# GATv2 and mixture-of-experts layer on one core: the norm's subtraction of one dropped, seven of the late message products moved from VectorE to GpSimd

## The chip, the cores and the metric

One core of one Trainium2 chip runs the whole kernel in one launch. The time is the device time of that core in microseconds (us). Times of separate runs are given as a median with the lowest and the highest run; one further execution was taken with the profiler, and all rows below are from that one.

## What is computed

The input is x of 1250 nodes by 256 features, and 40000 edges sorted by destination. Two residual steps follow each other; the change lies in the first, the graph step:

```python
def _gatv2_block(x, edge_index, W_l, W_r, att, bias, gamma, beta):   # x is already layer-normed
    xl = (x @ W_l).reshape(N, 4, 64);  xr = (x @ W_r).reshape(N, 4, 64)
    e = xl[src] + xr[dst];  e = where(e >= 0, e, 0.2 * e)
    score = einsum('ehd,hd->eh', e, att)
    ex = exp(score - segment_max(score, dst)[dst])
    alpha = ex / (segment_sum(ex, dst)[dst] + 1e-16)
    agg = segment_sum(alpha[:, :, None] * xl[src], dst)
    out = agg.reshape(N, 256) + bias
    h = elu(out) + x
    return (h - mean(h)) * rsqrt(var(h) + 1e-5) * gamma + beta
x = x + _gatv2_block(layernorm(x), ...)
x = x + top2_of_64_experts(layernorm(x))
```

The products alpha * xl[src] are called messages here. elu(out) is max(out, 0) + min(exp(out), 1) - 1.

## The kernel before, in words

The program runs in stages. The node stage norms x and projects it. The graph stage (`graph_phase`) goes over all edges. The route stage (`route_phase`) ends the sum with the bias, forms elu, norms twice, picks experts and scatters the rows to expert slots. The expert stage (`expert_phase`) does the two matrix products of 64 experts and adds up. The graph stage is a block of its own: no engine starts on the route stage before every engine has finished the graph stage.

The edges are cut in tiles of 128, and three tiles make a step: 108 steps (`STEPS`). Nine steps (`GPB`) make a block of the softmax, so there are 12 blocks, numbered 0 to 11. The last block but one is block 10, steps 90 to 98; the last block is steps 99 to 107. Each engine runs a loop over 108 + 20 loop steps (`STEPS + LAG`) with an order written out by hand:

- GpSimd only gathers: three indirect DMAs per step bring the rows xl[src] into the ring `G` of 26 steps (L131). The gathers for the last step are issued about 20 loop steps before the end; from then on GpSimd has nothing in the graph stage.
- TensorE at loop step s forms xl[src] + xr[dst] of step s in PSUM (`expand`, L689 to L696), turns the softmax's rows and columns of the block before (`turn_scores` to `turn_alpha`, L714 to L734), and aggregates step s - 20 (`aggregate`, L707): three matmuls by the one-hot matrix `M`, each of which the trace shows as two records, into `agg`, which fills five banks of PSUM. From loop step 108 there is nothing more to expand.
- ScalarE evacuates PSUM (L783, L784), takes the exponent of the scores (`exps`, L788), copies the weights alpha into `A` (`copy_alpha`, L794), and forms the third of a step's three messages, head by head (`weigh_head`, L805), one loop step ahead of TensorE.
- VectorE builds one-hots (L848), multiplies by att and reduces (L854, L862), runs the softmax of a block in pieces spread over loop steps k = 2 to 7 of the block after (`local_max` L904, L906, L890; `scan_rows` L896, L898; `full_max` L911 to L915; `local_sum` L920, L890, L922; `full_sum` L926 to L938), forms the first two of a step's messages in one 128x512 product (`weight`, L872), two loop steps ahead of TensorE, and scales the sum of the node that two blocks share (`rescale`, L881).

The ring `msg` holds four steps (`RA`), so the messages of step s may be written once step s - 4 is aggregated (semaphore `agged`). The order within one loop step of TensorE is fixed. At loop step 108 + k, k = 1, 2, 3, 5, 6 and 8, a turn for block 11 stands ahead of, or between, the aggregation of step 88 + k, and what stands behind a waiting turn waits too. In particular `turn_alpha` of block 11 stands ahead of the aggregation of step 96. The aggregation of the first step of a block waits for `rescale`.

Two chores were put in the last loop steps: ScalarE subtracts one from `xn`, the normed x, in five instructions of 128x512 (`lower`, L811 to L813, loop steps 109 to 113), and VectorE adds beta to xs in five (`add_beta`, L885). In the route stage `lift` adds min(exp, 1), max(out, 0) and `xn` (L1199 on GpSimd for all but the first of six groups, L1316, L1323), and the norm behind it subtracts the mean (L1301, L1304, L1332).

Of the kernel before, what the change touches and what calls it, by code (L numbers as in the profile page):

```python
# [23 lines left out]
P = 128  # L24
# [9 lines left out]
U = 3  # L34
# [30 lines left out]
LEAD = 2  # L65
CG = 3
# [473 lines left out]
def graph_phase(nc, v):  # L540
# [5 lines left out]
    with ExitStack() as ctx:  # L546
# [35 lines left out]
        consumed, freed = sem("consumed"), sem("freed")  # L582
        att_mul, scored, weighted, shared, agged = sem("att_mul"), sem("scored"), sem("weighted"), sem("shared"), sem("agged")
        dv = sem("dv_graph")
        init, rows_set, marks_out = sem("init"), sem("rows_set"), sem("marks_out")
# [16 lines left out]
        def by_block(row):  # L602

            return row.rearrange("o (b i) -> o b i", i=B)

# [59 lines left out]
        @block.gpsimd  # L665
        def _(g):

            for s in range(AHEAD, STEPS):
                if GS <= s < RG:
                    g.wait_ge(consumed, s - GS + 1)  # L670
                if s == RG - MG:
                    g.wait_ge(marks_out, 16 * 7)
                if s >= RG:
                    g.wait_ge(freed, s - RG + 2)
                gather_group(nc, G, xl_tab, srcI, gathered, s)

        @block.tensor
        def _(pe):
# [20 lines left out]
            def aggregate(s, u, w):  # L699

                if u == 0:
                    pe.wait_ge(weighted, s + 1)
# [34 lines left out]
            for s in range(STEPS + LAG):  # L737
# [3 lines left out]
                for u in range(U):  # L741
# [4 lines left out]
                    if (s, u) == (1, 0):  # L746
                        pe.wait_ge(init, 1)
# [23 lines left out]
        def _(act):  # L771
# [18 lines left out]
            def copy_alpha(b):  # L790
                act.wait_ge(alpha_ps, b + 1)
                if b >= 2:
                    act.wait_ge(weighted, GPB * (b - 1))
# [17 lines left out]
            def lower(i):  # L811

                nc.scalar.activation(xn[:, 2 * i:2 * i + 2, :], xn[:, 2 * i:2 * i + 2, :], ACT.Copy, bias=-1.0).then_inc(folded, 1)  # L813

            for s in range(STEPS + LAG):
                b, k = s // GPB - 1, s % GPB
                if 0 <= s - STEPS - 1 < NW // 2:
                    lower(s - STEPS - 1)
# [11 lines left out]
            act.wait_ge(folded, NW)  # L830

        @block.vector
        def _(dve):
# [31 lines left out]
            def weight(s):  # L865

                b, k, n = s // GPB, s % GPB, U - 1
                if k == 0:
                    dve.wait_ge(alpha_set, b + 1)
                if s >= RA:  # L870
                    dve.wait_ge(agged, s - RA + 1)
                V.tensor_tensor(msg[:, s % RA, 0:n * D].rearrange("p (q d) -> p q d", d=HD),  # L872
                                G[:, s % RG, 0:n * DX].rearrange("p (q f) -> p q f", f=HX)[:, :, 0:HD],
                                A[:, b % 2, k * U:k * U + n, :].rearrange("p u h -> p (u h)").unsqueeze(2)
                                .broadcast_to([P, n * HEADS, HD]), ALU.mult).then_inc(weighted, 1)
# [145 lines left out]
            dve.sem_inc(init, 1)  # L1021
            early = (clear_tables, mask_tables, end_tables, clear_marks, link_marks, row_marks, penalties, constants)

            for s in range(STEPS + LAG):
# [12 lines left out]
                if 0 <= s - LAG + LEAD < STEPS:  # L1037
                    weight(s - LAG + LEAD)
# [16 lines left out]
            dve.wait_ge(folded, NW)  # L1055
# [823 lines left out]
```

## Time and profile before

| | us |
|---|---|
| median of 3 runs | 880.72 |
| lowest and highest run | 874.63, 883.66 |
| the profiled execution, its own time | 872.36 |
| its span (first to last instruction) | 870.6 |
| TensorE busy in the span | 721.0 (83%) |
| VectorE busy | 560.3 (64%) |
| ScalarE busy | 355.9 (41%) |
| GpSimd busy | 411.5 (47%) |

The span starts at 0. PE is TensorE, PEld its weight loads, DVE is VectorE, ACT ScalarE, POOL GpSimd, SP SyncE. L872 is line 872 of the kernel. Busy time is a sum over a whole program with four stages, so it says nothing about one of them; the rows below are cut by time. The graph stage ends at about 622.6 us, and the part of it that the change touches begins at about 588 us.

### The profile page before, as it was taken

To read this page: it belongs to the slowest core of one execution; us is meant where nothing else is said; L and a number is where in the kernel's file an instruction comes from. 1 tells how busy PE (TensorE), PEld (TensorE's weight loads), DVE (VectorE), ACT (ScalarE), POOL (GpSimd) and SP (SyncE) were. 2 spreads that over 40 slices of the span, in tenths; PEclk is the share of its full clock that TensorE was granted. 3 is DMA by queue.
4 is the path that set the end of the run, shared out by engine and by line. 5 is a ranking of instruction groups with operands and counts; after the bars stand their busy time and mean duration, and the time that the engine had idled before them with its cause. 6 is when DMAs were issued, how large, how long until landed. Compare 5 with 4: busy or idle time off the path is not lost. (4 is left out here: it accounts for less than half of the span.)

```text
span 870.6 us, 14203 instructions
## 1 busy us (share of the span) xinstructions
PE 721.0 (83%) x4151; PEld 490.7 (56%) x4153; DVE 560.3 (64%) x1355; ACT 355.9 (41%) x1256; POOL 411.5 (47%) x405
## 2 busy tenths in 40 slices
PE   4844777997999889988988898998855499999995
PEld 2722444665666666666766565776544255555553
DVE  5653657886778777777876687878697333434333
ACT  1411334554455555555554464657632121121220
POOL 0566666366667656666765566710326011212121
PEclk9975798999999999999998899999955699999998
DMA  4545463344354435353534353510299899999995
GB/s 122 98 156 148 111 170 97 113 114 125 94 150 112 135 90 149 100 144 95 156 95 125 97 139 108 133 30 1 93 411 405 249 317 367 367 369 370 368 390 200
DMA packets 66875, 154.81 MB, mean 178 GB/s; under 512 B 17390, under 2 KB 30142, under 8 KB 66769
## 3 DMA queue, kind: packets, MB, share of 16 engines
q1 hardware_dynamic: 45824, 100.40, 34.2%
q0 software_dynamic: 18384, 51.06, 21.5%
q10 hardware_dynamic: 2592, 2.43, 0.9%
q8 instruction: 40, 0.66, 0.3%
q14 instruction: 35, 0.28, 0.1%
HBM read 138.76 MB, written 15.39 MB: 177 GB/s over the span
## 5 line engine op out<-in xcount | busy, mean ns | idle before, releaser
L131 POOL DMA_INDIRECT G<-xl_tab,srcI x324 | 344.6, 1064 | 196.0 <-issue 80.4
L783 ACT ACTIVATE L<-psE 128x264 f32<-128x264 f32 x324 | 126.4, 390 | 277.6 <-PE psE L696 200.0
L696 PE MATMUL psE<-G,ident 128*128 128x264 f32 x648 | 209.2, 406 | 0.0
L707 PE MATMUL agg<-msg,M 128*128 128x256 f32 x648 | 191.2, 395 | 6.4 <-issue 4.8
L693 PE MATMUL psE<-xr,MT 128*128 x972 | 176.9, 292 | 0.0
L854 DVE TENSOR_TENSOR L<-L,attb 128x792 f32<-128x792 f32 x108 | 105.7, 978 | 93.6 <-ACT M L784 46.5
L689 PE MATMUL psE<-identb,MT 128*128 128x128 bf16 x324 | 74.1, 229 | 81.4 <-issue 39.2
L805 ACT ACTIVATE msg<-G,A 128x64 f32<-128x64 f32 x432 | 136.8, 354 | 1.5 <-PE agg L707 1.2
L707 PEld LDWEIGHTS agg<-msg,M 128*128 128x128 f32 x648 | 118.5, 194 | 33.3 <-issue 17.4
L693 PEld LDWEIGHTS psE<-xr,MT 128*128 128x128 bf16 x972 | 88.5, 101 | 41.7 <-issue 6.0
L696 PEld LDWEIGHTS psE<-G,ident 128*128 128x128 f32 x648 | 105.5, 203 | 5.1
L862 DVE TENSOR_REDUCE S<-L 128x12 f32<-128x792 f32 x108 | 105.7, 978 | 3.4
L689 PEld LDWEIGHTS psE<-identb,MT 128*128 128x128 bf16 x324 | 32.7, 101 | 123.1 <-issue 65.3
L1612 POOL DMA_INDIRECT yk_d<-Y,row x33 | 31.7, 960 | 146.1 <-DVE Y L1769 133.7
L784 ACT COPY M<-psE 128x128 f32<-128x128 f32 x324 | 84.9, 262 | 0.0
L872 DVE TENSOR_TENSOR msg<-G,A 128x512 f32<-128x512 f32 x108 | 74.2, 687 | 2.5 <-PE agg L707 2.1
L1769 DVE COPY Y<-psY 128x256 f32<-128x256 f32 x32 | 13.6, 425 | 90.7 <-PE psY L1666 90.7
L1647 PE MATMUL psH<-w,xT 128*64 128x512 f32 x240 | 59.8, 620 | 0.0
L1661 PE MATMUL psY<-w,hid 128*64 128x256 f32 x480 | 57.0, 379 | 0.5 <-DMA w<-in_L_ffn_W 0.4
L1661 PEld LDWEIGHTS psY<-w,hid 128*64 128x64 f32 x480 | 34.3, 137 | 30.2 <-issue 15.4
L1828 ACT COPY hraw<-psH 128x512 f32<-128x512 f32 x33 | 19.3, 585 | 68.5 <-PE psH L1647 68.5
L1821 ACT COPY xT<-psXe 128x256 f32<-128x256 f32 x33 | 12.3, 372 | 70.8 <-PE psXe L1625 70.8
(302 smaller groups left out, 723.1 us busy)
## 6 DMA issues: line engine op xcount, KB each, us to landing
w<-in_L_ffn_W SPq DMA_DIRECT2D x120, 512.0 KB
relb<-rel_d SPq DMA_DIRECT2D x36, 288.0 KB
G<-xl_tab,srcI POOLq DMA_INDIRECT x324
tabs<-tab_d SPq DMA_DIRECT2D x48, 98.2 KB
X<-xs_d SPq DMA_DIRECT2D x58, 64.5 KB
xn<-in_L_ffn_W SPq DMA_DIRECT2D x6, 512.0 KB
h_in<-in_L_ffn_W SPq DMA_DIRECT2D x6, 512.0 KB
xs_d<-zslot SPq DMA_DIRECT2D x8, 322.5 KB
```

What stands on the lines that cost most here:

```text
L131: nc.gpsimd.indirect_dma_start(out=G[:, g % RG, u * DX:(u + 1) * DX], out_offset=None, in_=xl_tab, in_offset=bass.IndirectOffsetOnAxis(ap= ...
L689: turned = nc.tensor.matmul(psE[:, e, DX:DX + P], mt, identb[:, :], start=True, stop=True)
L693: nc.tensor.matmul(psE[:, e, 0:DX], mt, xr3[:, bass.ds(w * (3 * DX) + j * DX, DX)], start=(j == 0), stop=False)
L696: nc.tensor.matmul(psE[:, e, 0:DX], ident[:, :], G[:, s % RG, u * DX:(u + 1) * DX], start=False, stop=True).then_inc(expanded, 1)
L707: last = nc.tensor.matmul(agg[:, bass.ds(w * D, D)], M[:, s % RM, u * P:(u + 1) * P], msg[:, s % RA, u * D:(u + 1) * D], start=False, stop ...
L783: nc.scalar.activation(L[s % RL][:, u * DX:(u + 1) * DX], psE[:, e, 0:DX], ACT.Relu)
L784: nc.scalar.copy(M[:, s % RM, u * P:(u + 1) * P], psE[:, e, DX:DX + P]).then_inc(evacuated, 1)
L805: last = nc.scalar.activation(msg[:, s % RA, u * D + h * HD:u * D + (h + 1) * HD], G[:, s % RG, u * DX + h * HX:u * DX + h * HX + HD], ACT ...
L854: V.tensor_tensor(every, every, attb[:, :].unsqueeze(1).broadcast_to([P, U, DX]), ALU.mult).then_inc(att_mul, 1)
L862: V.tensor_reduce(S[:, b % 2, :, 1 + k * U:1 + (k + 1) * U].rearrange("p h u -> p u h"), L[s % RL][:, :].rearrange("p (u h f) -> p u h f", ...
L872: V.tensor_tensor(msg[:, s % RA, 0:n * D].rearrange("p (q d) -> p q d", d=HD), G[:, s % RG, 0:n * DX].rearrange("p (q f) -> p q f", f=HX)[ ...
L1661: last = nc.tensor.matmul(psY[part(h), b, 0:D], hid[:, b, m * P + h * CAP:m * P + (h + 1) * CAP], w2[2 * r + h][:, m, :], start=(m == 0), ...
```

## The change

Two edits. `lower` goes, and with it ScalarE's wait at its end; VectorE waits at the end of the stage for its own five `add_beta` alone. The route stage's text does not change: what it adds is now larger by one in every element, and the norm that follows subtracts the mean of the row. And for steps 92 to 98 (`BY_POOL`, the last seven of block 10) the 128x512 product of the first two messages is issued by GpSimd, behind its last gather, with a semaphore of its own (`weighted_p`), instead of by VectorE at loop steps 110 to 116. TensorE waits on the one or the other semaphore. ScalarE still forms the third message of every step. The semaphore `init` is replaced by a third count of `marked`. No DMA is added, removed or moved.

```diff
--- before.py
+++ after.py
@@ -63,6 +63,7 @@
 LAG = 20
 RM, RT, RL, RA = LAG + 2, 4, 3, 4
 LEAD = 2
+BY_POOL = range(STEPS - GPB - 7, STEPS - GPB)
 CG = 3
 CHUNKS, RC = STEPS // CG, 2
 assert STEPS % CG == 0 and RG - LAG <= GS and LAG >= 2 * GPB + LEAD
@@ -579,10 +580,10 @@
         colC, colD, colR, alphaT = psS[0:RB, 368:370], psS[0:RB, 370:372], psS[:, 372:372 + HEADS], psS[:, 384:384 + RB]
 
         onehot, expanded, evacuated = sem("onehot"), sem("expanded"), sem("evacuated")
-        consumed, freed = sem("consumed"), sem("freed")
+        consumed, freed, weighted_p = sem("consumed"), sem("freed"), sem("weighted_p")
         att_mul, scored, weighted, shared, agged = sem("att_mul"), sem("scored"), sem("weighted"), sem("shared"), sem("agged")
         dv = sem("dv_graph")
-        init, rows_set, marks_out = sem("init"), sem("rows_set"), sem("marks_out")
+        rows_set, marks_out = sem("rows_set"), sem("marks_out")
         tab_set, tab_out, marked, ends_in = sem("tab_set"), sem("tab_out"), sem("marked"), sem("ends_in")
         tabs_in = [sem(f"tabs_in{b}") for b in range(2)]
         scores_ps, ends_set, rows_ps, carried, cin_ps = map(sem, ("scores_ps", "ends_set", "rows_ps", "carried", "cin_ps"))
@@ -602,6 +603,18 @@
         def by_block(row):
 
             return row.rearrange("o (b i) -> o b i", i=B)
+
+        def pair_of_messages(eng, s):
+
+            b, k, n = s // GPB, s % GPB, U - 1
+            return eng.tensor_tensor(msg[:, s % RA, 0:n * D].rearrange("p (q d) -> p q d", d=HD),
+                                     G[:, s % RG, 0:n * DX].rearrange("p (q f) -> p q f", f=HX)[:, :, 0:HD],
+                                     A[:, b % 2, k * U:k * U + n, :].rearrange("p u h -> p (u h)").unsqueeze(2)
+                                     .broadcast_to([P, n * HEADS, HD]), ALU.mult)
+
+        def vector_messages(s):
+
+            return s + 1 - len([p for p in BY_POOL if p <= s])
 
         def load_tabs(sp, b):
 
@@ -673,6 +686,11 @@
                 if s >= RG:
                     g.wait_ge(freed, s - RG + 2)
                 gather_group(nc, G, xl_tab, srcI, gathered, s)
+            for s in BY_POOL:
+                if s == BY_POOL[0]:
+                    g.wait_ge(alpha_set, s // GPB + 1)
+                g.wait_ge(agged, s - RA + 1)
+                pair_of_messages(nc.gpsimd, s).then_inc(weighted_p, 1)
 
         @block.tensor
         def _(pe):
@@ -699,7 +717,10 @@
             def aggregate(s, u, w):
 
                 if u == 0:
-                    pe.wait_ge(weighted, s + 1)
+                    if s in BY_POOL:
+                        pe.wait_ge(weighted_p, s - BY_POOL[0] + 1)
+                    else:
+                        pe.wait_ge(weighted, vector_messages(s))
                     if s % GPB == 0 and s > 0:
                         pe.wait_ge(rescaled, s // GPB)
                 if u == U - 1:
@@ -744,7 +765,7 @@
                     if u == 0 and s + 1 < STEPS + LAG:
                         nxt = load_windows(pe, windows[(s + 1) % 2], wrow[0:1, s + 1, :])
                     if (s, u) == (1, 0):
-                        pe.wait_ge(init, 1)
+                        pe.wait_ge(marked, 3)
                         for j in range(NW * D // 512):
                             nc.tensor.matmul(agg[:, j * 512:(j + 1) * 512], zero[:, 0:P], zero[:, :], start=True, stop=False,
                                              skip_group_check=True)
@@ -790,7 +811,7 @@
             def copy_alpha(b):
                 act.wait_ge(alpha_ps, b + 1)
                 if b >= 2:
-                    act.wait_ge(weighted, GPB * (b - 1))
+                    act.wait_ge(weighted, vector_messages(GPB * (b - 1) - 1))
                 nc.scalar.copy(A[:, b % 2, :, :], alphaT.rearrange("p (h j) -> p j h", h=HEADS)[:, 1:BJ, :]).then_inc(alpha_set, 1)
                 act.wait_ge(alpha_set, b + 1)
 
@@ -808,14 +829,8 @@
                 if h == HEADS - 1:
                     last.then_inc(shared, 1)
 
-            def lower(i):
-
-                nc.scalar.activation(xn[:, 2 * i:2 * i + 2, :], xn[:, 2 * i:2 * i + 2, :], ACT.Copy, bias=-1.0).then_inc(folded, 1)
-
             for s in range(STEPS + LAG):
                 b, k = s // GPB - 1, s % GPB
-                if 0 <= s - STEPS - 1 < NW // 2:
-                    lower(s - STEPS - 1)
                 for u in range(U):
                     if s < STEPS:
                         evacuate(s, u)
@@ -827,7 +842,6 @@
                     if 0 <= s - LAG + 1 < STEPS:
                         for h in ((0,), (1,), (2, 3))[u]:
                             weigh_head(s - LAG + 1, h)
-            act.wait_ge(folded, NW)
 
         @block.vector
         def _(dve):
@@ -864,15 +878,11 @@
 
             def weight(s):
 
-                b, k, n = s // GPB, s % GPB, U - 1
-                if k == 0:
-                    dve.wait_ge(alpha_set, b + 1)
+                if s % GPB == 0:
+                    dve.wait_ge(alpha_set, s // GPB + 1)
                 if s >= RA:
                     dve.wait_ge(agged, s - RA + 1)
-                V.tensor_tensor(msg[:, s % RA, 0:n * D].rearrange("p (q d) -> p q d", d=HD),
-                                G[:, s % RG, 0:n * DX].rearrange("p (q f) -> p q f", f=HX)[:, :, 0:HD],
-                                A[:, b % 2, k * U:k * U + n, :].rearrange("p u h -> p (u h)").unsqueeze(2)
-                                .broadcast_to([P, n * HEADS, HD]), ALU.mult).then_inc(weighted, 1)
+                pair_of_messages(V, s).then_inc(weighted, 1)
 
             def rescale(b):
 
@@ -1018,7 +1028,7 @@
             c(V.memset(S[:, :, :, :], 0.0))
             c(V.memset(zero[:, :], 0.0))
             dve.wait_ge(dv, c.n)
-            dve.sem_inc(init, 1)
+            dve.sem_inc(marked, 1)
             early = (clear_tables, mask_tables, end_tables, clear_marks, link_marks, row_marks, penalties, constants)
 
             for s in range(STEPS + LAG):
@@ -1034,7 +1044,7 @@
                     firsts = load_windows(dve, [dve.alloc_register(f"first{i}") for i in range(wblk.shape[1])], wblk[0:1, :])
                 if 2 <= b <= NB and k == 0:
                     scale_column(b - 1)
-                if 0 <= s - LAG + LEAD < STEPS:
+                if 0 <= s - LAG + LEAD < STEPS and s - LAG + LEAD not in BY_POOL:
                     weight(s - LAG + LEAD)
                 if run and k in (3, 6):
                     scan_rows(b, k // 6)
@@ -1052,7 +1062,7 @@
                     score(s - 1)
                 if 0 <= s - STEPS - GPB - LEAD < NW // 2:
                     add_beta(s - STEPS - GPB - LEAD)
-            dve.wait_ge(folded, NW)
+            dve.wait_ge(folded, NW // 2)
             dve.wait_ge(agged, STEPS)
 
 
```

## Rows read from the trace of the kernel before

**Rows 1.** The page: the span, and the granted TensorE clock in 40 slices.

```profile
span 870.6 us, 14203 instructions
...
PEclk9975798999999999999998899999955699999998
```

**Rows 2.** Busy time by engine in four windows (window, length, then each engine).

```profile
core 0: us, PE busy (x) PEld busy (x) DVE busy (x) ACT busy (x) POOL busy (x), PEclk, DMA share, GB/s
588.00:605.00 17.00, 13.96 (x65) 9.84 (x64) 14.53 (x37) 11.68 (x43) 0.00 (x0) 1.00 0.00 0
605.00:610.00 5.00, 4.48 (x21) 3.49 (x21) 3.23 (x7) 4.44 (x19) 0.00 (x0) 1.00 0.01 3
610.00:622.50 12.50, 11.92 (x54) 10.18 (x54) 7.12 (x12) 6.97 (x27) 0.00 (x0) 1.00 0.00 0
```

**Rows 3.** TensorE's timeline, 588 to 623: start, length, line [idle before it].

```profile
588.39 2.06 PE L707 MATMUL agg<-msg,M 128*128 128x256 f32 x8
...
591.22 0.32 PE L716 MATMUL psS<-ident,S 128*112 128x128 f32 x1 [0.77 <-DVE S L862]
591.38 1.49 PE L707 MATMUL agg<-msg,M 128*128 128x256 f32 x6
...
594.12 1.99 PE L707 MATMUL agg<-msg,M 128*128 128x256 f32 x8 [0.77 <-DVE agg L881]
...
596.29 2.86 PE L707 MATMUL agg<-msg,M 128*128 128x256 f32 x12
599.37 0.26 PE L721 MATMUL psS<-ident,endc 112*1 112x112 f32 x1 [0.22 <-DVE endc L922]
...
604.95 0.38 PE L733 MATMUL psS<-rsel,one 112*128 112x4 f32 x2 [1.15 <-DVE X L938]
...
605.33 4.15 PE L707 MATMUL agg<-msg,M 128*128 128x256 f32 x18
610.31 11.92 PE L707 MATMUL agg<-msg,M 128*128 128x256 f32 x54 [0.83 <-DVE agg L881]
```

**Rows 4.** VectorE's timeline, 591 to 605.

```profile
591.08 0.68 DVE L872 TENSOR_TENSOR msg<-G,A 128x512 f32<-128x512 f32 x1
...
592.52 0.42 DVE L890 TENSOR_TENSOR_SCAN FT<-tabs,FT 112x128 f32<-112x128 f32 x1
...
595.71 0.69 DVE L872 TENSOR_TENSOR msg<-G,A 128x512 f32<-128x512 f32 x1 [0.69 <-PE agg L707]
...
597.36 0.29 DVE L915 SCALAR_TENSOR_TENSOR X<-FT,X 112x128 f32<-112x128 f32 x1
...
598.17 0.42 DVE L920 TENSOR_TENSOR_SCAN FT<-tabs,X 112x128 f32<-112x128 f32 x1
...
602.77 0.16 DVE L933 SCALAR_TENSOR_TENSOR rden<-endc,cin 112x1 f32<-112x1 f32 x1
...
604.60 0.29 DVE L938 TENSOR_TENSOR X<-X,FT 112x128 f32<-112x128 f32 x1
```

**Rows 5.** ScalarE: the exponent of block 11, and the instructions of `lower`.

```profile
597.68 0.31 ACT L788 ACTIVATE X<-X 112x128 f32<-112x128 f32 x1 [1.70 <-DVE X L915]
...
L813 ACT ACTIVATE xn<-xn x5: 615/621/624, 590.5 to 598.4; 128x512 f32<-128x512 f32 x5
```

**Rows 6.** Route stage: GpSimd's first two sums (min/median/max ns), VectorE beside and without them.

```profile
L1199 POOL TENSOR_TENSOR h_in<-h_in,xn x2: 1171/1414/1657, 625.7 to 627.4; 128x512 f32<-128x512 f32 x2
...
626.40 0.75 DVE L1301 BATCH_NORM_STATS2 stats<-ez 128x6 f32<-128x256 f32 x2
...
L1323 DVE SCALAR_TENSOR_TENSOR ez<-ez,h_in x2: 693/1137/1581, 625.7 to 627.5; 128x512 f32<-128x512 f32 x2
...
634.23 0.75 DVE L1301 BATCH_NORM_STATS2 stats<-xs 128x6 f32<-128x256 f32 x2
```

**Rows 7.** Two windows around a stall at 482 to 490 us, columns as in rows 2.

```profile
486.00:488.00 2.00, 0.69 (x2) 0.30 (x2) 0.00 (x0) 0.00 (x0) 0.87 (x1) 0.74 0.43 108
492.00:494.00 2.00, 2.00 (x8) 1.50 (x7) 1.51 (x5) 0.35 (x2) 0.13 (x1) 0.55 0.52 143
```

## The prediction, as made before the changed kernel ran

> **What bounds the kernel now.** I read the page's head first, to see that the granted clock is high where the change lies, in slices 27 and 28 of 40 (21.8 us each), and low in the three slices behind it [rows 1]. The page's chain that ended last stops at the start of the route stage, because every engine starts that stage together; so for this change the question is what ends the graph stage. For that I read windows, then the timelines of single engines.
>
> From 588 to 605 us TensorE is busy 13.96 of 17 us, VectorE 14.53, ScalarE 11.68, GpSimd not at all; from 610 to 622.5 TensorE is busy 11.92 of 12.5 [rows 2]. So there are two parts. In the second, 54 records (27 matmuls, steps 99 to 107) run without a gap: 11.92/9 = 1.32 us a step, which only TensorE sets. In the first, TensorE waits four times: 0.77 us for the scores, 0.77 for `rescale` of block 10, 0.22 for `endc`, 1.15 for the last product of the softmax, L938 [rows 3]. From `turn_alpha` at 604.95 on, everything is fixed: steps 96 to 98 in 4.15 us, the wait of 0.83 for `rescale` of block 11, steps 99 to 107. The end of the stage therefore moves by what L938 moves, as long as TensorE is not slower behind it. L938 ends at 604.60 + 0.29 [rows 4]. The whole question is what happens to VectorE's softmax of block 11 between 591 and 605 us.
>
> **Part 1: `lower` goes.** Five ScalarE instructions at 0.62 us [rows 5], some 3 us of ScalarE. What hides them: ScalarE waits 1.70 us for VectorE ahead of the exponent [rows 5], and its messages are formed a step or more ahead of TensorE, whose waits in rows 3 name VectorE each time and never ScalarE. The four that stand ahead of the exponent would cost only if VectorE came over 1.7 us earlier, and the fifth, behind it, delays only messages with slack. I take 0; the bounds are 0 and -0.62 (one of them, were it ever on the path; a loss is excluded since nothing is added). The `min`/`max` sums of the route stage keep their sizes, and the mean is subtracted there anyway: 0. `init` against `marked`: both are counted by VectorE at the same place, 0. The end wait of ScalarE falls on instructions done at 599: 0.
>
> **Part 2a: what leaves VectorE.** Seven products of 0.69 us that each take about 0.6 us of the queue, less the overlap with the next. Six of them (steps 92 to 97) stand between pieces of the softmax; the seventh stands behind L938 and gives nothing. Six times 0.6, with the idle 0.69 us in front of one of them (VectorE waits there for TensorE's aggregation [rows 4]), makes 4.3 us of VectorE's queue. But TensorE's turns stand in a fixed order between aggregations, so the softmax can't run faster than TensorE's queue. Worked through, with nothing else in the way: the scan L890 still ends at 592.94 [rows 4], since only the product for step 92 stood behind it. `rescale` then starts at once (aggregation of step 89 ends at 591.38 + 1.49 = 592.87 [rows 3]), 0.5 us earlier than before, so the eight records of 594.12 start at 593.6. Behind them the turn, twelve records of 2.86 us, and the turn of `endc`: TensorE reaches that turn at 598.7 where it ran at 599.37. VectorE is there in time (exponent 0.5 earlier and no product ahead of L920). Behind it TensorE's six records and the last turn set L926 as before. So the gain is the 0.5 us and the 0.2 us wait for `endc`: 0.65 us, not 4.3. That is the lower bound of the part, and the reason why little can be won here.
>
> **Part 2b: what comes to GpSimd.** Seven two-input products 128x512. The trace of before has none of `msg`, the nearest is L1199, a two-input sum 128x512: 1.17 us alone, 1.66 us when it was issued just after VectorE's L1323 [rows 6]. I take 1.17 us. GpSimd is free from its last gather on. Product 92 starts when step 88 is aggregated, at 588.39 + 2.06 = 590.45, so at about 590.55; each of the others when the step four before it is aggregated, that is about 1.3 us apart. TensorE needs each three steps (4 us) after that, so even 1.66 us apiece keeps them ahead. The added wait stands in TensorE's queue with all aggregations behind it, and costs 0.
>
> **Part 2c: two engines, one road.** L1323 on VectorE, two inputs in SBUF, 128x512, takes 0.69 us the first time, issued just ahead of GpSimd's first sum; the second time, at 627.5, some 0.1 us after GpSimd's second sum of 1.17 us had started, it took 1.58 us, so it lost 0.89 us, nearly all that was left of the other. VectorE's batch statistics, one input, take the same 0.75 us for two beside GpSimd's sum (626.40) and without it (634.23) [rows 6]. So a two-input VectorE instruction waits for the rest of a GpSimd product (less some 0.17 us), and the other way round.
>
> The Trainium skill (SBUF — State Buffer, "Who interferes with whom") puts it as an exclusive lock held for a whole instruction, which a VectorE instruction with two SBUF inputs contends for with a GpSimd instruction that reads SBUF; the second one to issue "fully blocks". This case's trace agrees with its 1.58 against 0.69 us. By that rule this move speaks against itself; by a rule of shared bandwidth each side would only be slowed in proportion.
>
> Which of VectorE's pieces have two SBUF inputs: the product for step 91, the scans L906, L920 and L890, L913, L915, L931, L933, L938. Those with a PSUM input (L904, L896, L898, L911, L926) have one. Now the walk with it:
> 1. Product 91 on VectorE is issued at 591.08 [rows 4], GpSimd's 92 runs 590.55 to 591.70: it ends some 0.45 us later than before. L890 then ends at 593.4, `rescale` at 593.75, TensorE's eight records start at 594.0, 0.1 us earlier than before in place of 0.5. (GpSimd's 93 becomes ready at 592.97, within 0.02 us of L890's issue. If it gets in first, add 1 us. I take it that it doesn't.)
> 2. The two L913 and L915 run 596.5 to 597.7 (the end of L915 from its row [rows 4]). GpSimd's 94 covers 595.6 to 596.75 and delays the first a little; 95 is ready when step 91 is aggregated, at 597.3, and gets in ahead of L915, which ends at 598.7 rather than 597.65: about 1.1 later than before in net.
> 3. The exponent follows, 0.31 us. GpSimd's 96 is ready at 598.65, and L920 comes at 599.1: it waits till 599.8. L920, L890 and L922 took 1.2 us to the turn at 599.37 [rows 3, 4]; the turn of `endc` comes at about 600.9, 1.5 us later.
> 4. L926 follows TensorE again, at 603.0. GpSimd's 97 ends at 603.35, ahead of L931. GpSimd's 98 is ready at 604.0 and gets in between L931 and L933, a chain of short dependent instructions: L933 at 604.25 waits till 605.3. From L933 on to the end of L938 it takes 604.89 - 602.77 = 2.1 us [rows 4]: L938 ends at 607.4, 2.5 us later than before.
>
> Bounds: -0.65 (no collision at all) and, if all seven products each block for 1.0 us, 7.0 - 0.65 = +6.4. I take the walk's +2.5, nearest to the row of 1.58 us.
>
> **Sum.** 0 + 2.5 us on the profiled execution: 872.36 + 2.5 = 874.9. The median of the runs shown lies 8.4 us above that execution, so I add the difference to the median: 880.7 + 2.5 = 883.2 us. About 1% (8.8 us) is what a measurement of this kernel tells from no change; the runs alone spread over 9.0 us.
>
> **The rivals.**
> A, the collisions don't fall on the softmax: the pieces of VectorE are short, and each lies between others that have one input; the order in which the two ask decides. For it: three of the seven products (93, 94, 97) hardly touch in my walk either. Against: four do. Time: the walk of 2a, 0.65 us less, 880.1. This one is not slower than before.
> B, the clock: a longer wait of TensorE lets the granted clock fall. For it: at 482 to 490 us, where TensorE had some 1.5 to 2 us idle at a time, the clock fell within 486 to 488 (mean 0.74, TensorE busy 0.69 of 2 us) and came back within 492 to 494 (mean 0.55) [rows 7], some 6 us at 1.2 GHz. Against: my walk has waits of 1.7 and 2.2 us with work between them, and the same stage has 1.00 at 13.96 of 17 us busy [rows 2]. Price: 6 us at half clock lose 3 us, once or twice: +2.5 + 3 to 6 = 5.5 to 8.5, some 888.
> C, GpSimd is much slower at this product than at L1199 (strided and broadcast inputs), over the 4 us that the ring gives: it decides from there on, and seven steps at 4 us in place of 1.32 would add up to 19 us, about 900. Against: the same number of elements, and no row of it near that.
>
> **How the numbers follow.** Forecast (a loss of 1 to 4 us) 0.50; A with its neighbours from -1 to +1 us 0.37; B 0.08; C 0.02; anything else, a gain from the earlier stages among it, 0.03. The bounds of the collisions alone make 880 to 887; with the spread of the medians of three (half of 9 us to each side) and part of B, the range is 876.5 to 888.5. Over 1% faster needs more than the stage has to give: 0.02. Over 1% slower is the upper part of B, and C: 0.05. Within 1%: 0.93.
>
> **What the profile after would show.** GpSimd: seven products, the first at about 590.5, 1.17 us or up to 1.7. VectorE between 591 and 607: product 91 near 1.1 us rather than 0.68, and some of L915, L920, L890, L933 well over their 0.16 to 0.42 us. TensorE: the wait ahead of L733 at about 2 us, L733 at about 607.4, then 4.15, `rescale`, 11.92 us as before, the last aggregation at about 624.7. ScalarE idle longer ahead of the exponent. I am wrong in 2c if VectorE's short pieces keep their lengths; wrong in 2a if L733 comes before 604.3; and B shows as a PEclk under 1.00 before 622.

## The result and the profile after

The changed kernel takes 878.12 us, median of 20 runs; the kernel before, run beside it, 876.31 us, median of 20. Taken run against run the ratio is 1.0051, with a 95% interval of 1.0026 to 1.0076: slower, by less than 1%. The ratio leaves out every run over 1.5% above the fastest of its own kernel: two of the changed kernel, at 1366 and 1770 us, and by that rule nine of the twenty of the kernel before, whose fastest, 865.00, is low (more in run 8). The two medians differ by 1.8 us, the ratio makes 4.5 us (2.3 to 6.7) of it. The time lies in the range, and the sign is the forecast one; 883.2 was 5 us too high, 4.4 of them because the 880.72 of three runs lay above the 876.31 that twenty give.

The profiled execution has a span of 873.8 us where before had 870.6. That difference must not be read as the cost. The last block's scores are turned at 591.22 before and at 594.99 after: 3.8 us in a part of the graph stage that the change does not touch. The gathers run there; what made these 3.8 us was not tried. So I measure inside the traces, from that turn: to the first matmul on `rsel` (`turn_alpha`), called the stretch below, and to the first matmul of the route stage. TensorE's timeline after, on the same columns as [rows 3]:

```profile
594.99 0.32 PE L737 MATMUL psS<-ident,S 128*112 128x128 f32 x1 [0.77 <-DVE S L876]
...
597.20 0.26 PE L742 MATMUL psS<-ident,FT 112*1 112x112 f32 x1 [0.56 <-DVE FT L900]
...
597.71 1.99 PE L728 MATMUL agg<-msg,M 128*128 128x256 f32 x8 [0.16 <-issue]
...
604.03 0.26 PE L742 MATMUL psS<-ident,endc 112*1 112x112 f32 x1 [1.29 <-DVE endc L932]
...
610.34 0.39 PE L754 MATMUL psS<-rsel,one 112*128 112x4 f32 x2 [1.86 <-DVE X L948]
...
610.72 4.16 PE L728 MATMUL agg<-msg,M 128*128 128x256 f32 x18
615.70 11.92 PE L728 MATMUL agg<-msg,M 128*128 128x256 f32 x54 [0.83 <-DVE agg L891]
628.45 7.66 PE L1223 MATMUL agg<-bg,one_r 1*128 1x512 f32 x10 [0.83 <-POOL one_r L1201]
```

The stretch is 610.34 - 594.99 = 15.35 us, against 604.95 - 591.22 = 13.73 [rows 3]: 1.62 us longer. TensorE's wait in front of it grew from 1.15 to 1.86, the one for `endc` from 0.22 to 1.29. Behind it everything has its old length: 4.16, 0.83, 11.92. The route stage starts 33.46 us after the scores' turn; before it was 31.83.

GpSimd's seven products, and VectorE at the same time (L610 is the product, by either engine; L868 to L953 are L854 to L943 of the kernel before):

```profile
594.38 1.04 POOL L610 TENSOR_TENSOR msg<-G,A 128x512 f32<-128x512 f32 x1 [20.16 <-PE agg L728]
596.72 1.25 POOL L610 TENSOR_TENSOR msg<-G,A 128x512 f32<-128x512 f32 x1 [1.30 <-PE agg L728]
599.35 1.04 POOL L610 TENSOR_TENSOR msg<-G,A 128x512 f32<-128x512 f32 x1 [1.38 <-PE agg L728]
601.10 1.06 POOL L610 TENSOR_TENSOR msg<-G,A 128x512 f32<-128x512 f32 x1 [0.70 <-PE agg L728]
602.39 1.04 POOL L610 TENSOR_TENSOR msg<-G,A 128x512 f32<-128x512 f32 x1 [0.23 <-PE agg L728]
605.35 1.04 POOL L610 TENSOR_TENSOR msg<-G,A 128x512 f32<-128x512 f32 x1 [1.91 <-PE agg L728]
607.26 1.04 POOL L610 TENSOR_TENSOR msg<-G,A 128x512 f32<-128x512 f32 x1 [0.87 <-PE agg L728]
```

```profile
594.85 1.12 DVE L610 TENSOR_TENSOR msg<-G,A 128x512 f32<-128x512 f32 x1
...
596.26 0.42 DVE L916 TENSOR_TENSOR_SCAN FT<-tabs,X 112x128 f32<-112x128 f32 x1
596.72 0.42 DVE L900 TENSOR_TENSOR_SCAN FT<-tabs,FT 112x128 f32<-112x128 f32 x1
...
600.97 0.29 DVE L925 SCALAR_TENSOR_TENSOR X<-FT,X 112x128 f32<-112x128 f32 x1
601.63 0.81 DVE L930 TENSOR_TENSOR_SCAN FT<-tabs,X 112x128 f32<-112x128 f32 x1 [0.38 <-ACT X L809]
602.47 1.24 DVE L900 TENSOR_TENSOR_SCAN FT<-tabs,FT 112x128 f32<-112x128 f32 x1
...
607.44 0.89 DVE L943 SCALAR_TENSOR_TENSOR rden<-endc,cin 112x1 f32<-112x1 f32 x1
```

Read the two together. Product 91 on VectorE, issued at 594.85 while GpSimd's 92 ran from 594.38 to 595.42, took 1.12 us in place of 0.68. The scan L900 at 596.72 was issued at the same moment as GpSimd's 93; the scan kept its 0.42 and the product took 1.25 in place of 1.04. L930 at 601.63 met product 95 (until 602.16) and took 0.81 in place of 0.42. L900 at 602.47 met 96 (from 602.39) and took 1.24 in place of 0.42: an excess of 0.82 of the 0.96 us that were left. L943, a sum of one number per partition, met 98 (until 608.30) and took 0.89 in place of 0.16. In all four VectorE lost 0.13 or 0.14 us less than what was left of the product. Every other piece has its old length, within 0.01 us. The excess of the three on the way to alpha is 0.39 + 0.82 + 0.73 = 1.94 us.

ScalarE had no part in it: it now waits 3.62 us ahead of the exponent, where before it waited 1.70 [rows 5].

```profile
601.29 0.31 ACT L809 ACTIVATE X<-X 112x128 f32<-112x128 f32 x1 [3.62 <-DVE X L925]
```

### The profile page after: what moved, and what is told of

The parts are those of the page before. It is cut to its first block and busy times, and to the rows that moved or that the text cites. A ratio compares the mean times of both kernels' runs of the same rounds, so it can differ in the third digit from the quotient of the medians.

```text
span 873.8 us, 14198 instructions
## 1 busy us (share of the span) xinstructions
PE 719.5 (82%) x4151; PEld 491.9 (56%) x4153; DVE 557.8 (64%) x1348; ACT 354.8 (41%) x1251; POOL 416.3 (48%) x412
## 3 DMA queue, kind: packets, MB, share of 16 engines
q10 hardware_dynamic: 2592, 2.43, 1.0%
## 5 line engine op out<-in xcount | busy, mean ns | idle before, releaser
L868 DVE TENSOR_TENSOR L<-L,attb 128x792 f32<-128x792 f32 x108 | 105.7, 978 | 107.6 <-ACT M L805 65.5
L610 DVE TENSOR_TENSOR msg<-G,A 128x512 f32<-128x512 f32 x101 | 69.8, 692 | 1.6 <-PE agg L728 1.2
L1671 PEld LDWEIGHTS psY<-w,hid 128*64 128x64 f32 x480 | 34.2, 137 | 30.1 <-issue 15.4
```

What stands on the lines that cost most here:

```text
L868: V.tensor_tensor(every, every, attb[:, :].unsqueeze(1).broadcast_to([P, U, DX]), ALU.mult).then_inc(att_mul, 1)
L1671: last = nc.tensor.matmul(psY[part(h), b, 0:D], hid[:, b, m * P + h * CAP:m * P + (h + 1) * CAP], w2[2 * r + h][:, m, :], start=(m == 0), ...
```

## The experiments

The theory: two-input VectorE instructions wait while GpSimd reads SBUF, and TensorE's fixed order lets the relief of VectorE give back only some 0.6 us. The rivals: the dropped subtraction plays a part; the hand-over to another semaphore costs in itself; VectorE's queue was the limit, so the relief is worth several us; what the ratio has over the stretch comes with the change in some other way (the clock in the route stage). The kernels ran on several chips, on which the graph stage differs by 70 to 100 us (the scores' turn at 492 to 504 us on two of them, at 573 to 595 on the others), so only the inside of the traces and the ratios taken on one chip are compared.

**1. The subtraction alone** (`e1_lower_only`), an edit of the kernel before.

```diff
-            def lower(i):
-                nc.scalar.activation(xn[:, 2 * i:2 * i + 2, :], xn[:, 2 * i:2 * i + 2, :], ACT.Copy, bias=-1.0).then_inc(folded, 1)
...
-                if 0 <= s - STEPS - 1 < NW // 2:
-                    lower(s - STEPS - 1)
...
-            act.wait_ge(folded, NW)
...
-            dve.wait_ge(folded, NW)
+            dve.wait_ge(folded, NW // 2)
```

> The kernel before with the subtraction of one (five ScalarE instructions) taken out, and nothing else. I measure the stretch from TensorE's turn of the last block's scores to the first matmul on rsel (turn_alpha): 13.73 us in the kernel before, 15.35 in the changed one. Theory (subtraction hidden): 13.7, times 1.000 of before. Rival (ScalarE was on the softmax's path after all): the stretch is shorter by 0.6 us or more.

Measured: stretch 505.56 - 491.83 = 13.73 us, and 31.83 us to the route stage, both as before to the hundredth. Ratio 1.0028 (0.9998 to 1.0058). The subtraction was hidden; in this stretch it is worth nothing. The ratio over 1 has no counterpart in the part that was edited; see run 8.

**2. The move alone** (`e2_pool_only`, the subtraction put back), an edit of the changed kernel.

```diff
+            def lower(i):
+                nc.scalar.activation(xn[:, 2 * i:2 * i + 2, :], xn[:, 2 * i:2 * i + 2, :], ACT.Copy, bias=-1.0).then_inc(folded, 1)
...
+                if 0 <= s - STEPS - 1 < NW // 2:
+                    lower(s - STEPS - 1)
...
+            act.wait_ge(folded, NW)
...
-            dve.wait_ge(folded, NW // 2)
+            dve.wait_ge(folded, NW)
```

> The changed kernel with the subtraction of one put back on ScalarE at its old places; so only the move of the seven products to GpSimd is left. Theory (VectorE's two-input pieces wait for GpSimd's products, ScalarE has room): stretch 15.3 us as in the changed kernel, time as the changed kernel's, 1.003 to 1.005 of before. Rival (ScalarE counts): the stretch comes out 0.6 us or more above 15.35.

Measured: stretch 15.36, to the route stage 33.46 us, ratio 1.0024 (0.9989 to 1.0059), a little under the expected 1.003. The move alone makes the whole 1.62 us. ScalarE still waits 1.54 us ahead of the exponent with the subtraction back in its queue.

**3. Nobody forms the products** (`e3_none`), an edit of the changed kernel.

```diff
-            for s in BY_POOL:
-                if s == BY_POOL[0]:
-                    g.wait_ge(alpha_set, s // GPB + 1)
-                g.wait_ge(agged, s - RA + 1)
-                pair_of_messages(nc.gpsimd, s).then_inc(weighted_p, 1)
...
-                    if s in BY_POOL:
-                        pe.wait_ge(weighted_p, s - BY_POOL[0] + 1)
-                    else:
+                    if s not in BY_POOL:
                         pe.wait_ge(weighted, vector_messages(s))
```

> The changed kernel in which nobody forms the seven products (the first two messages of steps 92 to 98 are left out, TensorE aggregates what stands in the ring). Theory (collisions make the loss, TensorE's fixed order limits the gain): no piece of the softmax over its length of before, product 91 back at 0.69 us, stretch 13.73 - 0.65 = 13.1 us. Rival (the stretch is longer because TensorE now waits or runs otherwise, whatever GpSimd does): stays near 15. Second rival (VectorE's queue, not TensorE's order, was the limit): near 13.73 - 3.6 = 10.1.

Measured: stretch 13.17 us, to the route stage 31.28 (the sums of these steps are wrong, since their products are left out). In VectorE's timeline all pieces have their old lengths:

```profile
503.06 0.42 DVE L923 TENSOR_TENSOR_SCAN FT<-tabs,X 112x128 f32<-112x128 f32 x1 [0.38 <-ACT X L802]
503.52 0.42 DVE L893 TENSOR_TENSOR_SCAN FT<-tabs,FT 112x128 f32<-112x128 f32 x1
...
507.66 0.16 DVE L936 SCALAR_TENSOR_TENSOR rden<-endc,cin 112x1 f32<-112x1 f32 x1
```

So the relief of VectorE, as if GpSimd's work were free, is worth 13.73 - 13.17 = 0.56 us, and the seven products on GpSimd cost 15.35 - 13.17 = 2.18 us. Of these, 1.94 are the three lengthened pieces; the other 0.25 is `rescale`, which product 91's 0.44 us had held back: TensorE goes on behind it 2.47 us after the scores' turn (499.14 - 496.67), in the changed kernel 2.72.

```profile
496.67 0.32 PE L730 MATMUL psS<-ident,S 128*112 128x128 f32 x1 [0.77 <-DVE S L869]
...
499.14 1.99 PE L721 MATMUL agg<-msg,M 128*128 128x256 f32 x8 [0.35 <-DVE agg L884]
```

The rival with VectorE's queue (10.1) is out by 3 us. VectorE now waits where its products stood, for TensorE's turns, 1.94 us ahead of L914: 

```profile
501.42 0.16 DVE L914 TENSOR_TENSOR cin<-psS,tabs 112x2 f32<-112x2 f32 x1 [1.94 <-PE psS L743]
```

**4. GpSimd writes but doesn't read** (`e4_writes`), an edit of the changed kernel.

```diff
-                pair_of_messages(nc.gpsimd, s).then_inc(weighted_p, 1)
+                nc.gpsimd.memset(msg[:, s % RA, 0:(U - 1) * D], 0.0).then_inc(weighted_p, 1)
```

> The changed kernel in which GpSimd's seven products are seven fills of the same 128x512 places with zero, at the same points and with the same semaphores: GpSimd writes SBUF but reads nothing (the products are left out). Theory (it is the reading of SBUF that blocks VectorE's second input): all pieces at their lengths of before, stretch 13.1 us. Rival (any GpSimd instruction on SBUF blocks VectorE's two-input pieces): pieces such as the scans and L943 are still lengthened, by up to the length of a fill (0.5 to 1 us each), stretch 13.5 to 14.5.

Measured: stretch 13.32 us, to the route stage 31.42; the theory had 13.1, its rival 13.5 or more. The fills keep the semaphores and the places of the products, and take 0.53 us each.

```profile
511.28 0.42 DVE L900 TENSOR_TENSOR_SCAN FT<-tabs,FT 112x128 f32<-112x128 f32 x1
511.74 0.38 DVE L932 TENSOR_SCALAR endc<-FT,q 112x2 f32<-112x2 f32 x1
...
515.57 0.16 DVE L943 SCALAR_TENSOR_TENSOR rden<-endc,cin 112x1 f32<-112x1 f32 x1
```

```profile
511.57 0.53 POOL L693 MEMSET msg<- 128x512 f32 x1 [0.77 <-PE agg L728]
...
515.38 0.52 POOL L693 MEMSET msg<- 128x512 f32 x1 [1.39 <-PE agg L728]
```

The hand-over costs nothing: waits and semaphores are those of the changed kernel, and 2.03 of the 2.18 us are gone. The remaining 0.15 us is one piece: L932, a scaling with one tensor input, 0.38 in place of 0.23 beside the fill. A fill is half as long as a product (0.53 against 1.04 us) and meets fewer pieces, so the stretch alone doesn't part reading from length. Nor does the scan at 511.28: it was running when the fill started, and a piece that starts first keeps its length beside a product too (L925, 0.29 us, in the changed kernel). What parts them is L943, with two inputs. It was issued at 515.57, when the fill had 0.33 us to go, and kept its 0.16; behind products, each such piece lost all but 0.13 or 0.14 us of what was left, which would be 0.2 us here. It is the only two-input piece that was issued well inside a fill, so this rests on one instruction. The Trainium skill (SBUF — State Buffer, "Who interferes with whom") has both halves: a VectorE instruction with two SBUF inputs contends with a GpSimd instruction that reads SBUF and not with one that only writes, and `tensor_scalar` can run in a mode of two ports that contends with either. This trace agrees, with the 0.16 us of L943 and the 0.38 of L932.

**5. Six products in place of seven** (`e5_six`), an edit of the changed kernel.

```diff
-BY_POOL = range(STEPS - GPB - 7, STEPS - GPB)
+BY_POOL = range(STEPS - GPB - 7, STEPS - GPB - 1)
```

> The changed kernel with six products on GpSimd (steps 92 to 97); the product for step 98 goes back to VectorE, behind the last piece of the softmax. Theory (each lengthened piece is one collision with one product): L943, 0.89 us in the changed kernel, is back at 0.16, the two scans keep their 0.81 and 1.24, and the stretch is 15.35 - 0.73 = 14.6 us. Rival (the loss is a general slowing of VectorE while GpSimd works): the stretch shrinks by a seventh of 1.62, to 15.1.

Measured: stretch 587.43 - 572.80 = 14.63 us.

```profile
579.45 0.81 DVE L930 TENSOR_TENSOR_SCAN FT<-tabs,X 112x128 f32<-112x128 f32 x1 [0.38 <-ACT X L809]
580.29 1.24 DVE L900 TENSOR_TENSOR_SCAN FT<-tabs,FT 112x128 f32<-112x128 f32 x1
...
585.25 0.16 DVE L943 SCALAR_TENSOR_TENSOR rden<-endc,cin 112x1 f32<-112x1 f32 x1
```

L943 is back at 0.16 and the stretch shorter by 0.72, its 0.73; the scans keep 0.81 and 1.24 on another chip. So each lengthened piece belongs to one product, and it is no general slowing.

**6. Each product twice** (`e13_twice`), an edit of the changed kernel.

```diff
                 pair_of_messages(nc.gpsimd, s).then_inc(weighted_p, 1)
+                g.wait_ge(weighted_p, 2 * (s - BY_POOL[0]) + 1)
+                pair_of_messages(nc.gpsimd, s).then_inc(weighted_p, 1)
...
-                        pe.wait_ge(weighted_p, s - BY_POOL[0] + 1)
+                        pe.wait_ge(weighted_p, 2 * (s - BY_POOL[0]) + 2)
```

> The changed kernel in which GpSimd forms each of the seven products twice, one behind the other, into the same place, and only then signals: the suspected cost doubled. Theory (VectorE's two-input pieces wait while GpSimd reads): GpSimd reads for some 2.1 us at a time, product 91 waits for it and more pieces meet one; stretch 17 to 20 us. Rival (the loss comes from the hand-over alone, the waits on other semaphores, with TensorE served in time since the ring holds four steps): about 15.4 us.

Measured: stretch 22.11 us, above the theory's range. VectorE's lengthened pieces are those with two inputs again, and more of them; new among them is L947, which scales `sel` by two numbers per partition and took 0.90 in place of 0.29:

```profile
503.45 2.10 DVE L925 SCALAR_TENSOR_TENSOR FT<-tabs,cin,FT 112x128 f32<-112x128 f32 x2
505.58 1.09 DVE L927 SCALAR_TENSOR_TENSOR X<-FT,X 112x128 f32<-112x128 f32 x1
...
515.21 0.90 DVE L947 TENSOR_SCALAR rsel<-sel,endc,rden 112x4 f32<-112x4 f32 x1
```

The rest is TensorE's clock, which the theory had not counted:

```profile
498.82 0.26 PE L744 MATMUL psS<-ident,FT 112*1 112x112 f32 x1 [1.68 <-DVE FT L902]
...
499.34 3.62 PE L730 MATMUL agg<-msg,M 128*128 128x256 f32 x8 [0.16 <-issue]
...
509.29 0.26 PE L744 MATMUL psS<-ident,endc 112*1 112x112 f32 x1 [3.29 <-DVE endc L934]
...
517.60 0.39 PE L756 MATMUL psS<-rsel,one 112*128 112x4 f32 x2 [2.47 <-DVE X L950]
```

```profile
500.00:502.00 2.00, 2.00 (x6) 1.55 (x6) 0.00 (x0) 0.00 (x0) 0.00 (x0) 0.50 0.00 0
502.00:504.00 2.00, 2.00 (x10) 1.26 (x9) 0.71 (x2) 0.00 (x0) 1.74 (x2) 0.76 0.00 0
...
510.00:513.00 3.00, 3.00 (x10) 2.00 (x9) 0.91 (x6) 0.35 (x2) 1.72 (x2) 0.50 0.00 0
```

The third number from the right is the granted clock (columns as in [rows 2]). Behind waits of 1.68 and 3.29 us it stood at 0.50 in two stretches, and the eight records of 1.99 us took 3.62. The six of 1.64 us behind the second wait took 2.50, and the ten of 2.43 behind them 2.86. The last 0.43 us of it stand ahead of TensorE's wait of 2.47 us for VectorE and cost nothing. Without the other 2.5 us the stretch would be about 19.6 us by this estimate, within the range. That is rival B of the prediction, in another kernel; in the changed kernel the clock stayed at 1.00 up to 628 us (see below). The length of a wait doesn't settle it: behind the 2.47 us the clock was 1.00 (517 to 523 us), and so it was behind the 1.86 us of the changed kernel, while 1.68 us here had 0.50 behind them. What does was not tried.

**7. A version without the collisions, and TensorE's order** (`e6_best`, `e10_best_again`, `e11_pool_late_alpha`). The first two are one kernel: the kernel before without the subtraction, all products on VectorE, put where VectorE waits (five of the seven) or behind the softmax's last piece (two); and for the last block `turn_alpha` stands two tiles later. The edit, on top of `e1_lower_only`:

```diff
-                        if (k, u) == (8, 0):
+                        if (k, u) == (8, 2 if b == NB - 1 else 0):
                             turn_alpha(b)
...
-                        if (k, u) == (8, 0):
+                        if (k, u) == (8, 2 if b == NB - 1 else 0):
                             copy_alpha(b)
...
-                if 0 <= s - LAG + LEAD < STEPS:
+                last = s >= STEPS
+                if 0 <= s - LAG + LEAD < STEPS and not (last and 2 <= k <= 8 and run):
                     weight(s - LAG + LEAD)
                 if run and k in (3, 6):
                     scan_rows(b, k // 6)
+                if run and last and k in (3, 6):
+                    weight(s - LAG + LEAD)
+                if run and last and k == 4:
+                    weight(s - LAG + LEAD)
...
                 if run and k == 7:
                     full_sum(b)
+                if run and last and k in (5, 7, 8):
+                    weight(s - LAG + LEAD)
...
                     rescale((s - LAG) // GPB)
+                if run and last and k == 2:
+                    weight(s - LAG + LEAD)
```

> The kernel before without the subtraction, all products on VectorE, but in the last loop steps each product stands where VectorE waits anyway (behind rescale at 110, behind the row scans at 111 and 114, behind local_sum at 113, behind full_sum at 115), and for the last block alone the turn of alpha and its copy stand two tiles later, after two aggregations of step 96. From the turn of the scores to the route stage's first matmul it is 31.83 us in the kernel before (623.05 - 591.22) and 33.46 in the changed one. Theory (TensorE's order is the limit): the products hide as in e3_none (-0.55 us) and TensorE fills its wait of 1.15 us ahead of alpha: 30.1 us. Rival (VectorE's queue sets it, or the later alpha comes too late for step 99): 31.3 or more. The time: 1.7 us less, 0.998 of before, hardly to be told from 1.

> e6_best again, for its time: from the scores' turn to the route stage 30.80 us (1.03 less than before, 2.65 less than the changed kernel), so 0.9988 of before; with the chance of the gathers 0.995 to 1.003.

`e11_pool_late_alpha` is the changed kernel with the first two hunks alone.

> The changed kernel with the turn of alpha and its copy of the last block two tiles later, as in e6_best. Theory (TensorE stands idle in front of this turn, and its order is a limit of its own beside the collisions): e6_best had 0.48 us from this; here the idle time is 1.86 us instead of 1.15, so two aggregations of 0.44 fill it fully: from the scores' turn to the route stage 33.46 - 0.88 + up to 0.41 given back = 32.6 to 33.0 us. Rival (the later alpha holds up step 99): 33.4 or more.

Measured, from the scores' turn to the route stage: 30.80 and 30.79 us for the first kernel, 32.98 for the second, against 31.83 before and 33.46 after. The products hide wholly (the stretch is 13.18 and 13.17, as when nobody formed them), and both kernels gain 0.48 us by the later turn. For the first I had expected the whole wait of 1.15 us (30.1 us in all); the second, for which I knew that, ended at the upper end of its 32.6 to 33.0. The rows of `e6_best` show why:

```profile
593.15 3.29 PE L707 MATMUL agg<-msg,M 128*128 128x256 f32 x14
596.72 0.39 PE L733 MATMUL psS<-rsel,one 112*128 112x4 f32 x2 [0.28 <-DVE X L931]
...
597.10 3.67 PE L707 MATMUL agg<-msg,M 128*128 128x256 f32 x14
```

Fourteen records take 3.29 us where nothing stops them; behind the turn they take 3.67. The wait ahead of the turn fell by 0.87 (1.15 to 0.28), and 0.4 of it came back there. What TensorE waits for in these 0.4 us the trace names only as "issue", and I leave it open. As a time the version can't be told from the kernel before: 0.9977 (0.9936 to 1.0018) and 1.0017 (0.9983 to 1.0051); its 1.03 us are 0.12%. That it beats both kernels is shown inside the traces alone.

**8. The excess of the ratio** (`e7_after_again`, `e8_before_again`, `e9_before_null`: the changed kernel, the kernel before, and the kernel before once more, each unedited).

> The changed kernel itself again, on this chip. If the excess over the 1.6 us of the stretch comes from the chance moment at which the clock falls in the route stage and from differences in the gathers ahead, the ratio lies between 1.001 and 1.005 with the stretch at 15.35, and the ten bias matmuls of the route stage (5.12 us in the kernel before, 7.66 in the changed one) take something else in 4.3 to 8.6 us. If the change itself makes the clock fall sooner, they stay near 7.7.

> The kernel before itself again, with its profile from this chip. Stretch 13.73 us again. If the moment of the clock's fall is chance, the ten bias matmuls take something else than 5.12 us, up to 8; if it goes with the kernel, they stay near 5.1 to 5.4, as in e1_lower_only.

> The kernel before, timed against itself: what the method makes of no change. Everything but chance says 1.000. If it comes out 0.2% or more off, the 1.0028 of e1_lower_only and what the changed kernel's 1.0051 has over the 1.6 us of the stretch (0.19%) are within what the method gives by chance; if it is within 0.1%, they stay unexplained.

Measured: stretch 15.35 for the changed kernel, 13.73 for both traces of the kernel before. The ten bias matmuls of the route stage took 7.49 us (changed), 7.14 and 7.62 us (before), against 7.66 (changed) and 5.12 (before) in the first two traces. They are long when the clock falls early in them:

```profile
629.00:630.00 1.00, 1.00 (x4) 0.42 (x3) 0.00 (x0) 0.39 (x1) 0.29 (x1) 0.87 0.29 66
630.00:631.00 1.00, 1.00 (x3) 0.48 (x2) 0.69 (x1) 0.20 (x1) 0.00 (x0) 0.50 0.46 129
```

That is the changed kernel's trace: the mean of 0.87 puts the fall at about 629.7, 1.3 us after their start at 628.45. In the first trace of the kernel before, where 626 to 627 us has a mean of 0.95, it came at about 626.9, 3.8 us after their start at 623.05. The same unedited kernel thus has anything from 5.1 to 7.6 us, so the moment is chance and no part of the change. Nor does it reach the end of the program. From their start to the end of the span it is 247.6 us (5.12), 246.0 (7.14) and 246.2 (7.62) for the kernel before, 245.4 (7.66) and 248.2 (7.49) for the changed one: no order in it.

The ratios: 1.0017 (0.9964 to 1.0071) for the changed kernel on that chip, and 1.0004 (0.9966 to 1.0041) for the kernel before against itself. The stretch explains 1.62 of 876 us, 1.0019. That lies inside the intervals of `e2_pool_only` and `e7_after_again`, and below the lower end, 1.0026, of the first measurement; the medians of that measurement, 1.8 us apart, would fit it. The null run is within 0.1%, so by what I wrote ahead of it the rest is unexplained. For the rest of 0.3%, some 3 us, I have found no place in the traces: the parts ahead of the scores' turn vary by more than that (four traces on one chip have it at 572.8 to 591.8 us), and `e1_lower_only`, whose edited part is equal to the hundredth, gave 1.0028 as well. The lists of runs show how little such a ratio can carry: taken over all runs but the two outliers, the means of the first measurement, 877.15 and 876.00 us, give 1.0013 (95%: about 0.998 to 1.0045) in place of 1.0051, and those of `e7_after_again` 1.0087 in place of 1.0017. Which runs are counted thus moves it by more than the 0.19% sought. That the change costs time is shown by the 1.62 us inside the traces; the rest of the ratio may be no more than this choice, and stays open.

## Why the prediction was right

- **Part 1, the subtraction at 0.** Right, shown by runs 1 and 2: 13.73 and 15.36 us with and without it.
- **Part 2a, relief worth 0.65 us and not 4.3, because TensorE's order sets the pace.** Right: 0.56 us in `e3_none`. This was the step that carried the sign. Without it the six products at 0.6 us would have read as a gain of some 4 us.
- **Part 2b, GpSimd's product at 1.17 us, always in time.** 1.04 us, and TensorE never waited for one. The first started 0.17 us after the aggregation it waits for, as good as predicted. Rival C is out.
- **Part 2c, collisions.** Right in kind; shown by `e3_none`, `e5_six` and `e13_twice`, and made narrower by `e4_writes`. In the walk, step 1 held: `rescale` let TensorE go on 2.72 us after the scores' turn, 0.18 us earlier than before where I said 0.1, and in the toss for L890 VectorE went first. Step 2 failed in its place: product 95 came 0.13 us after L915 had started, not ahead of it, so L915 kept 0.29; the product then met the scan L930 instead, 0.39 us in place of my 1.1. Step 3: 0.82 us in place of about 0.4 beyond it. Step 4: L933 (now L943), 0.73 in place of 1.05: the product took 1.04 us and not 1.17, and the walk let the piece lose all that was left, though 2c itself had measured some 0.17 us less than that. The pieces that were met are in part others than foretold: L915 not at all, but the scans L920 and L890 with 1.21 us together (0.39 and 0.82), where the walk had 0.7 for L920 alone. That the sum came as near as it did is in part luck. At the turn of `endc` it had 1.5 us, the traces have 0.89; at `turn_alpha` 2.5 and 1.62. The term mis-sized is the collisions, 3.1 us by my walk, 2.18 by the runs. The list of pieces that can collide was short, too: the two TENSOR_SCALAR pieces L922 and L935 of the kernel before are not on it, and were lengthened, the first beside a fill (run 4), the second beside a doubled product (run 6).
- **Rival A** (nothing collides, 0.65 us gained) is what `e3_none` looks like, not the changed kernel. **Rival B**: clock 1.00 through the whole tail, in two windows with the columns of [rows 2]:

```profile
588.00:610.00 22.00, 17.69 (x89) 12.88 (x88) 16.71 (x35) 11.84 (x48) 7.53 (x7) 1.00 0.01 1
610.00:628.00 18.00, 16.45 (x75) 13.72 (x75) 10.09 (x17) 11.41 (x45) 0.00 (x0) 1.00 0.00 1
```

  The chance given to it was not empty: `e13_twice`, with waits of 3.29 us for 1.29, has it.
- **Behind the stretch.** L754 to the route stage is 18.11 us, before 18.10: fixed, as said.
- **Not foreseen:** that the ratio, as it is taken, asks for some 3 us more than the stretch, and that the base of 880.72 would fall by 4.4 us with more runs. The time fell into the range in good part because the spread between runs had made it 12 us wide.

## What to carry to other kernels

Before you move work to an idle engine, ask two things of the trace: which engine's order sets the pace in that stretch (here TensorE's, so that clearing VectorE's queue of 4 us gave 0.6), and whether the two engines share a road to memory; here a two-input VectorE instruction issued beside a two-input GpSimd product waited for most of what was left of it, however short it was itself. Work that is in an engine's way can be moved into that same engine's waits: in `e6_best` the six products that had stood in the softmax's way cost nothing, five in VectorE's waits and one behind the softmax, without GpSimd. And where the effect is a thousandth of the time, measure a distance inside the trace: here it repeats to 0.01 us on every chip tried, while the ratio's interval is 0.25 to 0.5% wide to each side.

## What the runs showed of the hardware

- GpSimd's 128x512 f32 product of a strided and a broadcast input took 1.04 us, less than its contiguous 128x512 sum (1.17 us in [rows 6]).
- Of two instructions issued within 0.01 us (the scan and GpSimd's product at 596.72) one kept its length and the other took 0.21 us more; of those issued later, VectorE's lost 0.39 to 0.82 us of GpSimd's 1.04, each 0.13 or 0.14 us less than what was left of the product; L923, issued with 0.21 us left, lost 0.01. A sum of one number per partition (L943, 0.16 us) can lose 0.73 us, over four times its own length.
- A GpSimd fill with 0.33 us to go left a two-input piece alone (L943, 0.16 us), but one with 0.36 us to go took a scaling with one tensor input (L932) from 0.23 to 0.38 us.
- In one and the same kernel the granted clock fell at moments apart by over 2 us of the same code, with no trace of it in the time of the whole.
- Chips differ: the kernel before had medians of 777, 864 and 871 us on three of them, and the last block's scores were turned at 492 to 504 us on the first and at 573 to 594 on the others: the difference lies ahead of them, in the stages with the gathers. Each was seen once, so what makes the difference, chip or moment, was not tried.
